# Local attention with other orders on its engines, input loaded in pieces, silu moved into the last feed-forward, integer feed-forward written out

## The reference

```python
xn = layernorm(x); s = attn_i(xn); g = silu(ffn_i(xn)); x = x + s * g
```

```python
h = shift_token(x); q, k, v = split(h @ wqkv)          # 8 heads of 64
q = l2norm(q) * qs; k = l2norm(k) * ksc; q, k = rotary_xpos(q, k)
x = x + softmax(mask(8 * q @ k.T)) @ v @ wo             # window of 64, looks back one
h = layernorm(shift_token(x)) * lg + lb
a, g = split(h @ w1 + b1); x = x + (a * gelu(g)) @ w2 + b2
```

## Time and profile before

| | us |
|---|---|
| median of 3 runs (3312.03 to 3316.49) | 3316.05 |
| profiled execution | 3298.43 |
| its span | 3296.7 |
| start until the first matmul | 26.28 |
| integer feed-forward, first matmul to the next stage's | 899.08 to 1045.77 |
| local attention, steady part of the first layer | 1640 to 2270 |
| last gelu feed-forward ends, closing stage begins | 3269.0 |

### The profile page before, as it was taken

How to read it: one execution, slowest core, us unless ns; L and a number is a source line. 1 busy time by engine, 2 the same in 40 slices (tenths; PEclk the granted TensorE clock), 3 DMA queues, 4 the chain that set the end, 5 groups by cost and what they waited for, 6 DMA issues and landing times. The chain is left out here.

```text
span 3296.7 us, 64734 instructions
## 1 busy us (share of the span) xinstructions
PE 2889.4 (88%) x19916; PEld 1803.3 (55%) x19916; DVE 2272.7 (69%) x3245; ACT 2065.4 (63%) x5546; POOL 1041.8 (32%) x1162
## 2 busy tenths in 40 slices
PE   5799999988898699758699999998979999999896
PEld 3577987755533244426366666664435666666542
DVE  3666556666734589547688888884448888888545
ACT  3466656667523544333378778786847788877685
POOL 0233433310000034000255555552225555555320
PEclk9899999989899799879799999999989999999998
DMA  4200210000000000110000000000000000000001
GB/s 129 71 19 20 67 54 18 21 10 4 8 0 0 15 0 0 51 29 0 17 1 0 0 0 0 0 0 8 0 17 2 0 0 0 0 0 0 8 0 51
DMA packets 82856, 51.43 MB, mean 16 GB/s; under 512 B 28720, under 2 KB 75440, under 8 KB 82736
## 3 DMA queue, kind: packets, MB, share of 16 engines
q1 hardware_dynamic: 78640, 41.56, 4.5%
q0 software_dynamic: 4096, 8.40, 0.9%
HBM read 31.59 MB, written 18.35 MB: 15 GB/s over the span
## 5 line engine op out<-in xcount | busy, mean ns | idle before, releaser
L1840 PE MATMUL banks<-wqkv,hf 128*128 128x512 f32 x768 | 433.7, 648 | 77.6 <-ACT qt L1972 47.3
L1959 ACT ACTIVATE probs<-banks,minus_max,rnorm 128x128 f32<-128x128 f32 x1024 | 454.9, 465 | 3.1 <-DVE minus_max L2044 3.1
L1901 POOL TENSOR_TENSOR qk_cross<-qk_raw,rope_scaled 128x512 f32<-128x512 f32 x256 | 364.2, 1443 | 27.3 <-POOL hf L372 15.3
L1886 POOL TENSOR_TENSOR qk_rot<-qk_rot,rnorm 128x512 f32<-128x512 f32 x128 | 158.1, 1235 | 535.6 <-ACT rnorm L1996 528.6
L2074 DVE TENSOR_TENSOR qk_rot<-qk_raw,rope_scaled 128x512 f32<-128x512 f32 x256 | 292.7, 1183 | 22.9 <-ACT qk_raw L1989 22.9
L2024 DVE COPY probs_t<-banks 128x512 f32<-128x512 f32 x256 | 176.9, 691 | 89.6 <-PE banks L1818 85.4
L1959 ACT ACTIVATION_READ_ACCUMULATOR probs<-banks,minus_max,rnorm 128x1 f32 x1024 | 219.0, 214 | 0.0
L735 ACT ACTIVATE probs<-banks,minus_max 128x128 f32<-128x128 f32 (+1 forms) x512 | 207.9, 425 | 14.3 <-DVE minus_max L774 12.1
L1840 PEld LDWEIGHTS banks<-wqkv,hf 128*128 128x128 f32 x768 | 117.9, 193 | 138.4 <-issue 54.6
L1979 ACT ACTIVATE qk_raw<-banks 128x512 f32<-128x512 f32 x128 | 76.4, 597 | 174.8 <-PE banks L1840 174.8
L1832 PE MATMUL banks<-v_tok,probs_t 128*64 128x64 f32 x3072 | 174.6, 228 | 10.5 <-DVE probs_t L2024 10.5
(11 more groups left out here) (335 smaller groups left out, 7099.3 us busy)
## 6 DMA issues: line engine op xcount, KB each, us to landing
sorted_x<-zero_rows SPq DMA_DIRECT2D x10, 512.0 KB, 6.3
rows_in<-sorted_x SPq DMA_DIRECT2D x18, 256.0 KB, 3.1
sorted_y<-rows_out SPq DMA_DIRECT2D x18, 256.0 KB, 2.4
x_res<-in_x SPq DMA_DIRECT2D x8, 512.0 KB, 6.6
out_x<-x_res SPq DMA_DIRECT2D x16, 256.0 KB, 2.0
w1b<-in_L_ffn_w SPq DMA_DIRECT2D x8, 256.0 KB, 4.5
s_branch<-in_L_ffn_w SPq DMA_DIRECT2D x8, 256.0 KB, 6.2
w1g<-in_L_ffn_W SPq DMA_DIRECT2D x8, 256.0 KB, 3.0
```

What stands on the lines that cost most here:

```text
L1840: pe.matmul(ps[:, misc(k, j)], hf[:, n // 2 % 2, 0, n % 2 * P:(n % 2 + 1) * P], wqkv[:, w:w + QW], start=True, stop=True).then_inc(*S[name ...
L1886: pool.tensor_tensor(heads, heads, rn[:, (k + 2) % 4, 8:].unsqueeze(2).to_broadcast([P, HEADS, DH]), ALU.mult).then_inc(*S["unit"].inc)
L1901: last = pool.tensor_tensor(by_half(tw[:, n, at]), by_half(qk[:, n, at])[:, :, ::-1, :], tab[:, n, 2 * w + 1].rearrange("p (a d) -> p a d" ...
L1959: last = act.activation(pr[:, k % 2, head], ps[:, 2 * (k % 2) + par, c * P:(c + 1) * P], ACT.Exp, scale=rn[:, k % 4, head:head + 1], bias= ...
```

## The change

Five edits in one kernel.

1. **Input.** The 8 DMAs of `x` move into `start`, ahead of SP's semaphore bases, each with a semaphore of its own (`x0` to `x7`); the stage that loaded them goes. In `first_norm` PE waits for piece c // 2 before chunk c. The load of the two routing inputs is no stage of its own any more: SP issues it first in `first_norm`, waits for it, and PE (before its fifth chunk step) and DVE (before its first use) wait for it too.
2. **Integer feed-forward.** The loop becomes a written-out order like that of `gelu_ffn`: at step e PE runs down(e), up(e + 2), gate(e + 3). `silu_gate` and `hid` get three buffers. The silu of chunk c - 1 stands behind the second block of chunk c on ACT, its product and sum behind the third block on DVE.
3. **Local attention, DVE and POOL.** The straight part of tile k + 2 is made in slot k, behind the sum of squares, where that of tile k + 3 was made at the slot's end; the sum with the crossed part goes from between the two copies of probabilities to the slot's end; the first copy of probabilities goes ahead of the sum of squares. POOL runs scaling, crossed part, mix, shifted copy; the scaling is that of tile k + 1 (was k + 2), the crossed part that of k + 2 (was k + 3), and the second half of the crossed part waits for the row maxima of tile k. `qk_rot` gets four buffers (was two). PE's turn of q waits for `rotated` instead of `unit`.
4. **Local attention, ACT.** The copy of the turned q goes ahead of the squares.
5. **Silu in the last feed-forward.** `finish` goes. In the second `gelu_ffn` ACT makes tanh(xn / 2) of chunk c - 1 behind the gelu of the second block, DVE makes (tanh + 1) * xn, times `s`, times 0.5 plus `x` behind the third block, and SP stores the chunk.

```diff
@@ start
+            for k in range(8):
+                at = slice(k * (N // 8), (k + 1) * (N // 8))
+                sp.dma_start(m["x"][:, at], a["x"][:, at]).then_inc(S[f"x{k}"].sem, 16)
             for step in [step for step in S.values() if step.base]:
                 sp.sem_inc(step.sem, step.base)
...
-    load(nc, [(m["x"][:, k * (N // 8):(k + 1) * (N // 8)], a["x"][:, k * (N // 8):(k + 1) * (N // 8)]) for k in range(8)])
@@ first_norm
-        load(nc, [(both[:, P:], a["L0_ffn_switch_w"]), (sb[:], a["L0_ffn_switch_b"].partition_broadcast(P))])
+                for dst, src in early:
+                    sp.dma_start(dst, src).then_inc(S["loaded"].sem, 16)
+                sp.wait_ge(*early_in)
...
+                        pe.wait_ge(S[f"x{c // 2}"].sem, 16)
@@ integer_ffn
+                for e, c, f in steps():
+                    if e >= 0:
+                        pe.wait_ge(*S["gated"].at(0, e))
+                        if f == 0:
+                            pe.wait_ge(*S["silu"].at(0, c - 2))
+                        pe.matmul(ps[:, OUT_AT + c % 2], w[:, 2, f * P:(f + 1) * P], hd[:, e % 3], start=(f == 0),
+                                  stop=(f == FT - 1)).then_inc(*S["down"].inc)
+                    if 0 <= e + 2 < FT * R:
+                        u = e + 2
+                        pe.wait_ge(*S["gated"].at(0, u - 2))
+                        pe.matmul(ps[:, 2 * (u % 2)], w[:, 1, u % FT * P:(u % FT + 1) * P], m["xn"][:, tokens(u // FT)],
+                                  start=True, stop=True).then_inc(*S["up"].inc)
+                    if 0 <= e + 3 < FT * R:
+                        u = e + 3
+                        pe.wait_ge(*S["act_a"].at(0, u - 2))
+                        pe.matmul(ps[:, 2 * (u % 2) + 1], w[:, 0, u % FT * P:(u % FT + 1) * P], m["xn"][:, tokens(u // FT)],
+                                  start=True, stop=True).then_inc(*S["gate_ps"].inc)
@@ local_attention, PE: pe_turn_qk
-            pe.wait_ge(*S["unit"].at(i, n))
+            pe.wait_ge(*S["unit" if name == "kt" else "rotated"].at(i, n))
@@ local_attention, POOL: slot
+                    if here(i, k + 2):
+                        pool.wait_ge(*S["q_sb"].at(i, k + 2))
+                        pool.wait_ge(*S["k_sb"].at(i, k + 2))
+                        pool.wait_ge(*S["rotated"].at(i, k))
+                        cross(i, k, 0)
+                        if here(i, k):
+                            pool.wait_ge(*S["rowmax"].at(i, k))
+                        cross(i, k, 1).then_inc(*S["crossed"].inc)
@@ gelu_ffn, ACT
+                def sigmoid(c):
+                    act.wait_ge(*S["added"].at(0, c))
+                    act.wait_ge(*S["both"].at(0, c - 2))
+                    act.activation(gate[:, c % 2], m["xn"][:, c * C:(c + 1) * C], ACT.Tanh, scale=0.5).then_inc(*S["tanh"].inc)
...
+                    if out is not None and f == 1 and c >= 1:
+                        sigmoid(c - 1)
@@ gelu_ffn, DVE
+                def finish(c):
+                    at = slice(c * C, (c + 1) * C)
+                    dve.wait_ge(*S["tanh"].at(0, c))
+                    dve.scalar_tensor_tensor(gate[:, c % 2], gate[:, c % 2], 1.0, m["xn"][:, at], ALU.add, ALU.mult)\
+                        .then_inc(*S["fused"].inc)
+                    dve.wait_ge(*S["fused"].at(0, c))
+                    dve.tensor_tensor(gate[:, c % 2], gate[:, c % 2], m["s"][:, at], ALU.mult).then_inc(*S["weighed"].inc)
+                    dve.wait_ge(*S["weighed"].at(0, c))
+                    dve.scalar_tensor_tensor(m["x"][:, at], gate[:, c % 2], 0.5, m["x"][:, at], ALU.mult, ALU.add)\
+                        .then_inc(*S["both"].inc)
...
+                    if out is not None and f == 2 and c >= 1:
+                        finish(c - 1)
                 add(R - 1)
+                if out is not None:
+                    finish(R - 1)
```

More of the change, by code:

```diff
@@ L103 @@
 POOL_MOVES = ["moved0", "moved1"]
+X_MOVES = [f"x{k}" for k in range(8)]
 def cols(i, u, width, parts=2):
@@ L122, in build @@
             STEPS[n] = Step(ctx.enter_context(nc.semaphore(n)), 16)
+        for n in X_MOVES:
+            STEPS[n] = Step(ctx.enter_context(nc.semaphore(n)), 16)
+            STEPS[n].base = 0
         for n in POOL_MOVES:
@@ L151, in build @@
             local_attention(nc, ps, m, a, layer)
-            gelu_ffn(nc, ps, m, a, layer)
-        finish(nc, m, out)
+            gelu_ffn(nc, ps, m, a, layer, out if layer == DEPTH - 1 else None)
 def on_chip(nc, mem):
@@ L224, in column @@
     return vec.rearrange("(p o) -> p o", o=1)
[L227 to L255, removed]
-                sp.wait_ge(S["stored"].sem, 16 * (PRIME + 2 * R))
-def add_gated(dve, m, gate, i, u):
-    S = STEPS
-    dve.wait_ge(*S["silu"].at(i, u))
-    dve.tensor_tensor(gate[:, u], gate[:, u], m["s"][:, cols(i, u, C)], ALU.mult).then_inc(*S["weighed"].inc)
-    dve.wait_ge(*S["weighed"].at(i, u))
-    dve.tensor_tensor(m["x"][:, cols(i, u, C)], m["x"][:, cols(i, u, C)], gate[:, u], ALU.add)\
-        .then_inc(*S["added"].inc)
 def layer_norm(nc, ps, m, src, dst, affine=None, shifted=False):
@@ L1271, in integer_ffn, with tokens, steps @@
                    a["L1_ffn_w_down"].rearrange("(f p) d -> p f d", p=P))])
-        with Stage(R, up=2 * FT, act_a=2 * FT, gated=2 * FT, m1=2 * FT, silu=2, weighed=2, added=2), nc.Block() as block:
+        def tokens(c):
+            return slice(c * C, (c + 1) * C)
+        def steps():
+            for e in range(-FT, FT * R):
+                yield e, e // FT, e % FT
+        with Stage(1, prep=2, gate_ps=FT * R, up=FT * R, act_a=FT * R, gated=FT * R, down=FT * R, silu=R, weighed=R,
+                   added=R), nc.Block() as block:
@@ L1324, in scan_mixer @@
+                for e, c, f in steps():
+                    if e >= 0:
+                        dve.wait_ge(*S["act_a"].at(0, e))
+                        dve.wait_ge(*S["up"].at(0, e))
+                        dve.wait_ge(*S["down"].at(0, e - 3))
+                        dve.tensor_tensor(hd[:, e % 3], sg[:, e % 3], ps[:, 2 * (e % 2)], ALU.mult).then_inc(*S["gated"].inc)
+                    if f == 2 and c >= 1:
+                        add(c - 1)
+                add(R - 1)
 def scan_mixer(nc, ps, m, a):
@@ L2108, in gelu_ffn @@
         with Stage(1, copied=R, mean=R, centered=R, squared=R, variance=R, logged=R, deviation=R, scaled=R, normed=R,
-                   gate_ps=FT * R, up=FT * R, gelu=FT * R, gated=FT * R, down=FT * R, added=R), nc.Block() as block:
+                   gate_ps=FT * R, up=FT * R, gelu=FT * R, gated=FT * R, down=FT * R, added=R,
+                   **{name: R * (out is not None) for name in ("tanh", "fused", "weighed", "both")}), nc.Block() as block:
             @block.sync
@@ L2114, in _ @@
                 sp.wait_ge(*ready)
+                if out is not None:
+                    for c in range(R):
+                        sp.wait_ge(*S["both"].at(0, c))
+                        sp.dma_start(out[:, c * C:(c + 1) * C], m["x"][:, c * C:(c + 1) * C]).then_inc(S["stored"].sem, 16)
+                    sp.wait_ge(S["stored"].sem, 16 * (PRIME + R))
             @block.gpsimd
```

162 lines of the change are left out of this document (76 added, 86 removed).

## The result

The changed kernel takes 3201.3 us (median of 4 runs, 3200.7 to 3202.5), the kernel before, run beside it, 3315.6: ratio 0.966, 95% interval 0.964 to 0.967, 114 us less. The profiled execution takes 3200.86, its span 3198.5.

The account below looks back on a forecast made before the run. Four places were to count: PE's late start, the integer feed-forward's chunks, a closing stage without PE work, and the nearly full local attention. 12.4 + 15 + 21 + 36 = 84 us less, 3316 to 3232; range 3205 to 3273.

Parts of the forecast that it names:

- The local attention: Largest of the four places: 0.31 us less a slot over 128 slots, 36 us less after longer first slots and waits.
- The change leaves this chain alone: Local attention, start of q's product (T) to v's (V): ACT's chain there, 4.06 and 4.28 us, stays unchanged.
- DVE's new order costs something: Local attention: DVE idles 1 us ahead of the first probability copy; the second ends 5.6 us after q's product starts.
- From V to T: Local attention, v's product to the next q's: 5.65 and 5.64 us; ACT's exchange saves 0.38, 0.31 after a 0.07 charge.
- The tie: Local attention: DVE's second copy and PE's arrival for it nearly coincide, 5.7 against 5.55 or 5.77 us; 0.07 charged.
- The first slots: Local attention: they get longer by the straight pair that is not made ahead, 1.4 us a layer.
- The straight pair held up: Rival, local attention: DVE's straight products wait for POOL and delay the second copy; up to 3366 us; chance 0.12, slower 0.04.
- The start: Input loads issued earlier: PE starts at 13.9 us instead of 26.28, 12.4 us less, bounds 11 to 13.
- The integer feed-forward: 15 chunks go from 8.79 to 7.72 us, less 1.1 for the last block: 15 us less, bounds 10 to 17.
- The closing stage: Silu work moved into the last feed-forward: the end comes at 3275.7, 21 us earlier, bounds 15 to 22.
- The table rule: Counter-argument, last feed-forward: tanh outside gelu's table set adds two 1.28 us loads a chunk, giving back about 15 of 21 us.
- The base: Whole kernel: median of runs lies 17.6 us above the profiled execution, in unnamed stages; the 84 us are taken from the median.

Follow-up runs that it names:

- The single exchange on DVE: Kernel before with only DVE's first copy of turned probabilities moved ahead of the sum of squares: 3296.6 us against 3316.3, ratio 0.994.
- moving the second copy: Changed kernel with DVE's second copy of turned probabilities between the two straight products instead of behind both: 3160.8 us against 3295.3 for the kernel before, ratio 0.960.
- the run with silu: Changed kernel with ACT's own silu for tanh in the last feed-forward, and two buffers for three in the integer feed-forward: 3217.8 us, ratio 0.970 to the kernel before.
- two exchanges: Kernel before with only ACT's turned-q copy ahead of the squares and DVE's first probability copy ahead of the sum of squares: ratio 0.980.

## Why the prediction was wrong

The sign, the four places and three of the terms held; the time was 31 us too long. Point by point:

- **The local attention** is the step that failed: "The change leaves this chain alone", from T to V, and "DVE's new order costs something". Both were read from two slots of four. In the long one the old order of DVE held PE (0.72 us), so DVE's new order shortened that stretch by 0.24 on average. The single exchange on DVE shows it: T to V 4.34 to 4.13, 19.7 us less. The slot of before is 9.91, not 9.81, that of after 9.40, not 9.50, and 0.5 x 128 is the 64 us.
- **From V to T** the forecast has 5.34 (5.65 less 0.31) and the changed kernel 5.33, but by luck: three errors cancel. The two slots read have 5.65 and 5.64, all four 5.57 on average. The exchange on ACT was put at 0.38; beside DVE's new order, with the second copy out of the way, it is worth 0.46 (5.62 to 5.16), and alone 0.51. The tie was seen but under-priced: 0.07 charged, while moving the second copy showed 0.17 a slot lost to it. What is left for ACT's order in the changed kernel is 0.29, for the 0.31 said.
- **The first slots** were to get longer; the second of each stage is 2 us shorter (11.19 to 9.22).
- **The straight pair held up** did not happen: 690 ns, as expected against this rival. The Trainium skill, SBUF — State Buffer, section on who interferes with whom, was cited for the exclusion of the two engines, with the sum of the two parts beside POOL's shifted copy as the next place. The trace agrees: in the slot above the sum starts at 1868.78 and takes 1.24, and the second half of that copy, begun at 1868.98, takes 1.30, where it took 0.40 alone in a slot of before. That happens to 27 of the 64 copies, while 35 take 0.40. The sum takes 1.21 to 1.25 in 111 of 128 cases, otherwise up to 1.43. From 1640 to 2140 us PE stands idle for neither:

```profile
1868.78 1.24 DVE L2077 TENSOR_TENSOR qk_rot<-qk_rot,qk_cross 128x1024 f32<-128x1024 f32 x1
...
1868.98 1.30 POOL L335 COPY hf<-xn 64x255 f32 x1
```

- **The start** is right: 13.7 for 13.9.
- **The integer feed-forward**: chunks of 7.72 as said. It gave 17.0 and not 15, since no wait appeared in the last block and the first chunk got a little shorter too. The layernorm behind it, put at nothing, gave 4.5 in this pair. Its first 20 us had a granted clock of 0.77 before and 1.00 after (the third figure; the second is PE's busy time):

```profile
1045.70:1065.00 19.30, 17.28 (x30) 0.77 0.00 1
```

```profile
1037.40:1057.00 19.60, 17.59 (x40) 1.00 0.00 1
```

  Over the profiles it is 102.7 to 103.1 with the old feed-forward, in six of them, and 98.1 to 102.1 with the new one, in eight. The new order ahead does not settle it: with the second copy between the straight products and without POOL's wait the same feed-forward stood ahead, the granted clock of these 20 us was 0.76, and the stage took 101.9 and 102.1. What decides it is not shown.
- **The closing stage**: 19.1 for 21. The last sum is held by the finish of chunk 14 as forecast (0.75, for 0.92), and from its start to the end it is 6.0 and not 6.5 (half of that is a slip: the terms given add up to 3273.0, not 3273.2). Another 2.6 us are lost at the stage's start, where PE was at the lower clock longer (granted clock 0.88 from 3041 to 3055 us, 0.99 in the same stretch of the stage before). That is not the edit's: from first to last product the stage takes 161.5 to 164.1 with the closing stage of before as well, 164.1 in the run with the one exchange on DVE, with the same 0.88. In the chunks with layernorm the distance is 9.44 in both layers, with the three more instructions and without. **The table rule**: tanh needed no load, and the run with silu shows what two loads a chunk cost, 18 us where I had said about 15. The Trainium skill, ScalarE: Activation LUTs, section on table sets, names gelu's set without tanh; read as a rule, that would have brought the same loads with tanh. The trace has none of them: 104 loads in the changed kernel, 105 before, 135 with silu.
- **The base**: "in stages that I can't name". As far as the profiles show it is one stage. The latent attention, the same code in all kernels, took 454 to 461 us in the profiles of the two comparisons in which the kernel before ran at 3298.5 and 3295.3, and 470 to 476 in those of the one in which it ran at 3316.3. The profile of before (457.8) is of the first kind, the changed kernel (479.2) of the second, and so are, by their time, the timed runs of before. Taking the difference from the median was right.

## What to carry to other kernels

In a loop with four slots a round, read all four before pricing one: the slot that differs is the one with the slack to gain, and two neighbours showed nothing of it. Where two engines tie, an exchange on one alone moves the wait to the other; price it with the other's chain at the new pace, and look for the instruction on it that nobody needs yet. Then undo the parts one by one: here two exchanges, out of five edits, gave what all the attention's edits gave together. When two versions come out equal, compare the stretches too: here each lost on one what it gained on the other.

## What the runs showed of the hardware

The latent attention, unchanged code, differed by some 20 us between comparisons, and no other stage differed so. The three comparisons ran on three chips, each at its own time, so it may be the chip or not. The first of its two parts, from PE's first product to that of the next stage, before and after:

```profile
107.08 1.19 PE L643 MATMUL banks<-xf,wk_lat 128*128 128x256 f32 x2 [11.59 <-POOL xf L712]
...
334.61 1.12 PE L957 MATMUL banks<-ident,rows_in 128*128 128x128 f32 x4 [4.51 <-DMA rows_in<-sorted_x]
```

```profile
94.76 1.19 PE L615 MATMUL banks<-xf,wk_lat 128*128 128x256 f32 x2 [11.58 <-POOL xf L684]
...
335.35 0.90 PE L929 MATMUL banks<-ident,rows_in 128*128 128x128 f32 x3 [6.17 <-DMA rows_in<-sorted_x]
```

That is 227.5 and 240.6 us. PE is 99% busy there or more in both (209.3 and 207.2 us of 210, from 110 to 320), so the idle times of the profile don't name a cause. It was not tried what sets it.
